# The MLP's read of tiles 4 to 15 made by GpSimd and VectorE in place of TensorE

## The reference, cut to what matters

```python
def rat_read(res, W, gamma, beta, num_outputs):      # MLP: num_outputs = 2
    x = res.reshape(b, l, H, C)                      # H = 512, C = 4
    y = jnp.einsum('blhc,hoc->bloh', x, W)           # sums of four products
    mu = y.mean(-1, keepdims=True)
    var = y.var(-1, keepdims=True)
    yn = (y - mu) * jax.lax.rsqrt(var + EPS)
    yn = yn * gamma + beta                           # per output and column
    return yn.reshape(b, l, num_outputs * H)
```

```python
delta = softplus(delta_low @ du_w.T + du_b)
A_bar = exp(delta * A_neg)                           # 1536 per token
hidden = hs * A_full + out * B_full                  # 2048 per token
```

## Time and profile before

| | us |
|---|---|
| three timed executions | 1629.28, 1638.53, 1634.19 |
| their median | 1634.19 |
| span of the profiled execution | 1627.3 |
| median less span | 6.9 |

### The profile page before, as it was taken

The page is one execution under the profiler, slowest core; times in us unless marked ns, Lnnn a source line. Parts: engine busy times, 40 slices in busy tenths (PEclk is TensorE's granted clock), DMA queues, the critical chain, the costliest instruction groups (busy, mean ns, idle before and its releaser), DMA issues.

```text
span 1627.3 us, 25328 instructions
## 1 busy us (share of the span) xinstructions
PE 1531.8 (94%) x9574; PEld 1169.6 (72%) x9574; DVE 1129.6 (69%) x1782; ACT 921.9 (57%) x1702; POOL 364.1 (22%) x346
## 2 busy tenths in 40 slices
PE   7999999999999988899999999899999999999986
PEld 6567666666666656778798778798877898875554
DVE  7777745888888878644463785974776955636777
ACT  5444345888888776455543656643657644552443
POOL 1645555555433420110002000012000011001000
PEclk8999999999999999899999999999999999999998
DMA  9667677999987945356577766667766667756542
GB/s 371 204 254 243 223 181 229 276 293 284 273 233 197 253 138 189 130 185 223 202 218 233 258 226 221 214 218 232 265 233 221 223 197 237 218 180 213 203 178 104
DMA packets 127609, 360.94 MB, mean 222 GB/s; under 512 B 15744, under 2 KB 45056, under 8 KB 111872
## 3 DMA queue, kind: packets, MB, share of 16 engines
q1 hardware_dynamic: 127200, 359.19, 68.7%
q10 hardware_dynamic: 288, 0.13, 0.0%
HBM read 273.15 MB, written 86.11 MB: 221 GB/s over the span
## 4 chain that ended last, share of the span: by engine, by line
PE 74%; DVE 12%; ACT 6%; DMA 3%; issue 3%; POOL 1%; SPq 0%; DVEq 0%; ACTq 0%; POOLq 0%
PE ps L1921 21%; PE ps L1933 9%; PE ps L693 5%; PE ps L1249 5%; PE ps L1236 4%; PE ps L1272 4%; PE ps L1946 4%; PE ps L1879 3%; PE ps L1864 3%; PE ps L1809 3%; ACT a_p L1378 3%; PE ps L1824 3%; PE ps L1891 3%; DMA p_x<-in_x 2%; PE ps L652 2%
## 5 line engine op out<-in xcount | busy, mean ns | idle before, releaser
L1921 PE MATMUL ps<-m_y_split,m_win 128*128 128x512 f32 x1536 | 372.7, 396 | 2.7 <-issue 2.7
L1921 PEld LDWEIGHTS ps<-m_y_split,m_win 128*128 128x128 f32 x1536 | 284.2, 189 | 63.9 <-issue 7.1
L1308 DVE TENSOR_REDUCE a_negmax<-ps 128x1 f32<-128x640 f32 (+7 forms) x176 | 180.7, 1027 | 61.1 <-PE ps L1239 60.3
L1378 ACT ACTIVATE a_p<-ps,a_negmax 128x128 f32<-128x128 f32 (+7 forms) x256 | 188.5, 750 | 36.0 <-DVE a_negmax L1308 33.8
L1933 PE MATMUL ps<-m_wods,m_y_split 128*128 128x316 f32 x768 | 178.7, 322 | 3.8 <-DVE m_hT L2145 3.4
L2183 ACT ACTIVATE m_turned<-ps 128x512 f32<-128x512 f32 x128 | 75.0, 596 | 160.3 <-PE ps L1809 129.1
L1249 PE MATMUL ps<-ident,a_p 128*128 128x128 f32 x1152 | 157.8, 275 | 2.9 <-DVE a_pT L1321 2.0
L1236 PE MATMUL ps<-a_k,a_q 128*128 128x512 f32 (+3 forms) x384 | 124.4, 403 | 16.7 <-ACT a_p L1378 15.0
L1933 PEld LDWEIGHTS ps<-m_wods,m_y_split 128*128 128x128 f32 x768 | 128.5, 192 | 8.0 <-DVE m_hT L2145 3.7
L1249 PEld LDWEIGHTS ps<-ident,a_p 128*128 128x128 f32 x1152 | 123.5, 141 | 5.4 <-DVE a_pT L1321 3.5
L2341 POOL TENSOR_TENSOR m_scale<-m_scale,mhalf 128x2 f32<-128x2 f32 x16 | 13.0, 813 | 493.5 <-DVE m_scale L2081 493.5
(11 more groups left out here) (250 smaller groups left out, 3095.3 us busy)
## 6 DMA issues: line engine op xcount, KB each, us to landing
m_win<-mlp_in_split SPq DMA_DIRECT2D x128, 512.0 KB, 4.4
m_wods<-mlp_out_split SPq DMA_DIRECT2D x96, 316.0 KB, 3.3
p_xT<-in_xT SPq DMA_DIRECT2D x16, 1024.0 KB, 9.9
p_x<-in_x SPq DMA_DIRECT2D x16, 1024.0 KB, 10.6
a_q<-qk_split SPq DMA_DIRECT2D x64, 256.0 KB, 7.0
a_k<-qk_split SPq DMA_DIRECT2D x128, 128.0 KB, 7.2
mlp_in_split<-a_w_two SPq DMA_DIRECT2D x32, 512.0 KB, 5.5
m_hs<-in_x SPq DMA_DIRECT2D x15, 1024.0 KB, 5.6
```

Source lines behind the costliest of these rows:

```text
L1308: V.tensor_reduce(negmax[:, n % 4, 0:len(units[n][3])], by_head(n, score_banks(n)), AX_X, ALU.max, negate=True).then_inc(max_ready, 1)
L1378: m = S.activation(dst[:, j, :], src[:, j, :], ACT.Exp, bias=negmax[:, n % 4, j:j + 1], accum_out=rsum[:, si % 2, q * 4 + hh:q * 4 + hh + 1])
L1921: m = nc.tensor.matmul(bank_of("m", blk, step), win[s][:, wl, ic, :], y[k], start=(ic == 0 and p3 == 0), stop=(ic == HCH - 1 and p3 == 2))
```

## The change

For tiles 4 to 15 the parts turn0 to turn3 and read0 to read3 go; fold0 to fold3 come in, two MLP steps apart. In fold q GpSimd multiplies quarter q of the tile (512 columns, repeated for both outputs by a zero step) with the weights `wide2[q]`, which lie in SBUF repeated over all partitions, and puts the 1024 products in `Ab[0]`; VectorE sums fours into `y2`. GpSimd's product q waits for VectorE's sum q - 1, and VectorE's sum q for GpSimd's product q. The statistics and the normalisation then work on `y2` in SBUF, in pieces of 512 columns. Tiles 0 to 3 keep the old way. The weights `wide2` are 4 KB a partition for each quarter: three loads of 512 KB in the attention stage, and one at the load of tile 4, over `read2`. To make room, the scratch that the program reserves for DMA descriptors is given as 1024.

```diff
-       'turn0': 13.72,
-       'turn1': 14.22,
-       'read0': 15.22,
-       'read1': 15.23,
-       'turn2': 15.72,
-       'turn3': 16.91,
-       'read2': 17.94,
-       'read3': 17.95,
+       'fold0': 11.2,
+       'fold1': 13.2,
+       'fold2': 15.2,
+       'fold3': 17.2,
        'stats': 17.96,
        'norm': 18.88},
...
+            for q in (1, 2, 3):
+                load_wide(q)
+
+        def load_wide(q):
+            move(wide2[q][:, :, :], read2_rows[q].unsqueeze(0).broadcast_to([P, RD2, BLK])).then_inc(wide_loaded, 16)
...
+        def folds_of(i):
+            return 4 * (i - TB + 1) if i >= TB else 0
...
             if step == "outer":
                 dve.wait_ge(dve_own.sem, own_at[what, i])
+                if lane_before[what, i] and lane_before[what, i][0] == "a":
+                    dve.wait_ge(folded, folds_of(lane_before[what, i][1]))
...
+            if part == "fold":                                  # write_dve
+                c = i % TB
+                dve.wait_ge(widened, folds_of(i) - 3 + q)
+                V.tensor_reduce(y2[c][:, :, P * q:P * q + P],
+                                Ab[0][:, 0:RD2 * BLK].rearrange("p (o h c) -> p o h c", o=RD2, c=C), AX_X,
+                                ALU.add).then_inc(folded, 1)
+            if part == "stats" and i >= TB:
+                c = i % TB
+                dve.wait_ge(folded, folds_of(i))
+                for o in range(RD2):
+                    n = dve_own.then_inc(V.bn_stats(m_st[:, c, o, 0, :], y2[c][:, o, :]))
...
             if part == "norm":                                  # write_act
                 c = i % TB
                 act.wait_ge(yscale2_ready, i + 1)
-                act.wait_ge(turn2_mm, 8 * (i // TB))
+                if i >= TB:
+                    for o in range(RD2):
+                        m = S.activation(y2[c][:, o, :], y2[c][:, o, :], ACT.Identity, bias=m_sc[:, c, 2, o:o + 1],
+                                         scale=m_sc[:, c, 1, o:o + 1])
+                    m.then_inc(y2_ready, 1)
+                    return
...
+            if part == "fold":                                  # write_pool
+                c = i % TB
+                if q == 0:
+                    pool.wait_ge(hs_ready, nth("sum", what, i))
+                    pool.wait_ge(wide_loaded, 64)
+                    pool.wait_ge(turn2_mm, 8 * (i // TB))
+                x4 = hs[hs_of[what, i]][:, BLK * q:BLK * q + BLK].unsqueeze(1).broadcast_to([P, RD2, BLK])
+                pool.wait_ge(folded, folds_of(i) - 4 + q)
+                G.tensor_tensor(Ab[0][:, 0:RD2 * BLK].rearrange("p (o f) -> p o f", o=RD2), x4, wide2[q][:, :, :],
+                                ALU.mult).then_inc(widened, 1)
...
             if part == "load":                                  # write_sp
+                if (what, i) == ("a", TB):
+                    for q2 in (2, 3):
+                        wait_for_quarter(sp, "a", TB - 1, q2)
+                    load_wide(0)
                 if hs_before[what, i]:
                     kind, j = hs_before[what, i]
                     if kind == "a":
-                        sp.wait_ge(turnq_mm, quarter["a", j, 3] + 1)
+                        if j < TB:
+                            sp.wait_ge(turnq_mm, quarter["a", j, 3] + 1)
+                        else:
+                            sp.wait_ge(folded, folds_of(j))
                         sp.wait_ge(hs_stored[h], stored["a", j])
...
-    nc = bacc.Bacc("TRN2", target_bir_lowering=False, num_devices=1)
+    nc = bacc.Bacc("TRN2", target_bir_lowering=False, num_devices=1, dynamic_dma_scratch_size=1024)
```

More of the change, by code:

```diff
@@ L262, in program @@
             read1_in, gamma1_in, beta1_in, qkvT, wod1T, wab1_b, du1_rows,
-            read2_in, gamma2_in, beta2_in, mlp_inT, wod2T, wab2_b, du2_rows,
+            read2_in, read2_rows, gamma2_in, beta2_in, mlp_inT, wod2T, wab2_b, du2_rows,
             expA, expB, br, out):
@@ L418, in program @@
         place[0] = ring_end
+        read2_place = place[0]
         read2 = sb("m_read2", [P, DCH, RD2, HPC])
+        read2_end = place[0]
         gam2 = sb("m_gamma2", [P, RD2 * HCH])
@@ L445, in program @@
         m_sc = sb("m_scale", [P, TB, 3, RD2])
+        wide2 = []
+        after, place[0] = place[0], read2_place
+        wide2.append(sb("m_read2_wide0", [P, RD2, BLK]))
+        assert place[0] == read2_end
+        place[0] = after
+        wide2 += [sb(f"m_read2_wide{q}", [P, RD2, BLK]) for q in (1, 2, 3)]
         place[0] = keep
@@ L536, in program @@
         emptied = sems("bank_emptied", 8)
-        rep1_loaded, rope_in_loaded, causal_loaded, wq_loaded, wkv_loaded = (
-            sem(n) for n in ("rep1_loaded", "rope_in_loaded", "causal_loaded", "wq_loaded",
+        rep_loaded, rope_in_loaded, causal_loaded, wq_loaded, wkv_loaded = (
+            sem(n) for n in ("rep_loaded", "rope_in_loaded", "causal_loaded", "wq_loaded",
                              "wkv_loaded"))
@@ L566, in program @@
         raw_loaded, two_stored, two_ready = sems("raw_loaded", 4), sems("two_stored", 3), sem("two_ready")
-        const2_loaded, rep2_loaded, du_loaded, du_ready = (
-            sem(n) for n in ("const2_loaded", "rep2_loaded", "du_loaded", "du_ready"))
+        const2_loaded, du_loaded, du_ready = (
+            sem(n) for n in ("const2_loaded", "du_loaded", "du_ready"))
         oT_loaded, hs_loaded, mx_loaded = sems("oT_loaded", 4), sems("hs_loaded", 6), sems("mx_loaded", 2)
@@ L585, in program @@
             sem(n) for n in ("y2_ready", "turn2_mm", "yhi_ready", "ylo_ready"))
+        wide_loaded, widened, folded = sem("wide_loaded"), sem("widened"), sem("folded")
         wt_loaded = sems("wt_loaded", NW)
@@ L729, in project_dve @@
             n48 = DCH * RD1
-            dve.wait_ge(rep1_loaded, 32)
+            dve.wait_ge(rep_loaded, 32)
             each = n48 // 3
@@ L1036, in project_sp @@
         def project_sp():
-            move(p_spread[:, :], spread_in).then_inc(rep1_loaded, 16)
-            move(wrep1[:, :], read1_in).then_inc(rep1_loaded, 16)
+            move(p_spread[:, :], spread_in).then_inc(rep_loaded, 16)
+            move(wrep1[:, :], read1_in).then_inc(rep_loaded, 16)
             def load(i):
@@ L1558, in prepare_sp @@
             move(bet2[:, :], beta2_in).then_inc(const2_loaded, 16)
-            move(m_spread[:, :], spread_in).then_inc(rep2_loaded, 16)
-            move(wrep2[:, :], read2_in).then_inc(rep2_loaded, 16)
+            move(m_spread[:, :], spread_in).then_inc(rep_loaded, 16)
+            move(wrep2[:, :], read2_in).then_inc(rep_loaded, 16)
             for k, wab in enumerate((wab1_b, wab2_b)):
@@ L1586, in prepare_dve @@
             n32 = DCH * RD2
-            dve.wait_ge(rep2_loaded, 32)
+            dve.wait_ge(rep_loaded, 64)
             V.tensor_tensor(read2[:, :, :, :].rearrange("p a b c -> p (a b) c"),
@@ L2068, in write_dve @@
                 V.tensor_tensor(hs[h][:, :], hs[h][:, :], m_x[x_at][:, :], ALU.add).then_inc(x2_ready, 1)
-            if part == "stats":
+            if part == "fold":
[9 more added lines that the diff above has]
+                    n = dve_own.then_inc(V.bn_stats(m_st[:, c, o, 0, :], y2[c][:, o, :]))
+                dve.wait_ge(dve_own.sem, n)
+                for o in range(RD2):
+                    n = dve_own.then_inc(V.bn_aggr(m_my[:, c, o, :], m_st[:, c, o, 0, :]))
+                dve.wait_ge(dve_own.sem, n)
+                V.tensor_scalar(m_sc[:, c, 0, :], m_my[:, c, :, 1], EPS, None, ALU.add).then_inc(yvar2_ready, 1)
+            if part == "stats" and i < TB:
                 c = i % TB
@@ L2411, in write_sp @@
                 move(m_x[x_at][:, :], x[i]).then_inc(mx_loaded[x_at], 16)
-            if part == "turn" and q == 0:
+            if part in ("turn", "fold") and q == 0:
                 sp.wait_ge(hs_ready, nth("sum", what, i))
@@ L2529 @@
         "read2": read_rep(L0_xattn_mlp_read_w, RD2),
+        "read2_rows": lay(np.transpose(np.reshape(L0_xattn_mlp_read_w, (4, P, RD2, C)), (0, 2, 1, 3)).reshape(4, RD2, BLK)),
         "gamma2": lay(np.reshape(L0_xattn_mlp_read_g, (RD2 * HCH, P)).T),
```

## The result

The changed kernel takes 1697.53 us (median of 4 runs, 1696.40 to 1700.18), the kernel before 1636.36 (4 runs, 1629.28 to 1638.54): 61 us slower, ratio 1.039, 95% interval 1.037 to 1.042. The profiled execution took 1697.61 with a span of 1695.5. The matmuls that the change takes away are gone, and the time went up all the same: with the 58 us of the prediction's first term, some 119 us were given back.

A forecast was written before the change was run, and what follows sets the result against it. TensorE was taken as the bound, VectorE next and on the path in dense stretches. Span 1627.3 - 19.4 + 3 - 2 - 2 = 1606.9, plus 6.9 to the runs' median: 1614 us, range 1587 to 1648.

The forecast's parts named there:

- What is removed: 58 us: First term: TensorE loses transposes and products in tiles 4 to 15, 4.8 us a tile, twelve tiles 58 us.
- GpSimd's product 2.38 us, VectorE's sum 1.2: Added per fold in tiles 4 to 15: a 1024-column product (taken 2.4 us) and a 1024-column sum (1.2 us).
- The two engines against each other: The lock: GpSimd's product holds VectorE's next operation with two SBUF inputs, up to 2.4 us a fold, 9.6 a tile.
- The sign that the prediction named for the lock: If right, VectorE's L1992 and L2021 to L2033 would show a mean above 1.76 us.
- The assumption on PSUM: VectorE operations that read PSUM keep their times while a GpSimd product runs.
- Smaller edits: SyncE at 0: SyncE's load of the next x behind fold3 costs 0, at most 4 us at tiles 10 and 14.
- The sums: 2 x 4.8 charged in dense places: VectorE's four sums, 4.8 us a tile, counted where VectorE is the path, at tiles 10 and 14.
- the waits for the product, charged only at tile 7: Tile 7's chain of folds ends late, so TensorE waits 2.4 us, taken as 3, before the first turn.
- Block 0: -16.4: Tiles 4 to 7: VectorE's free time covers the folds, -19.4 us, with 3 us of waiting after tile 7.
- Blocks 1 and 2: -2 each: Tiles 8 to 11 and 12 to 15: -19.4 + 2 + 12.8 + 2.7 = -2 us each.
- Rival 2: VectorE's in-order queue becomes the path in blocks 1 and 2; four dense tiles pay: +20, 1654 us, chance 0.25.

The follow-up runs named there:

- x12: Changed kernel with fold products and sums on a few columns, SyncE's store back at 13.72, load of the next x left at 4.08: 1589.6 us, ratio 0.973.
- x8: Changed kernel with only tiles 4 to 7 read by folds, products on VectorE, SyncE's store at 13.72 and load at 5.5, scratch 128: 1617.8 us, ratio 0.989.
- x4: Changed kernel with each GpSimd product replaced by two fills about as long that read nothing from SBUF: 1643.9 us, ratio 1.006.
- x13: Changed kernel, folds whole, with SyncE's store back at 13.72 and the load left at 4.08: 1683.9 us, ratio 1.030.
- x14: x8 with the load of the next x back at 4.08: 1617.7 us, ratio 0.990.
- x3: Changed kernel with GpSimd's products on 8 columns an output, the sums whole: 1634.4 us, ratio 1.000.
- x1: Changed kernel with products on 8 columns and 2 sums an output, same places and waits: 1618.6 us, ratio 0.991.
- x7: Changed kernel with only tiles 4 to 7 read by folds, products on GpSimd, SyncE's store at 13.72 and load at 5.5, scratch 128: 1626.5 us, ratio 0.995.
- x6: Changed kernel with VectorE making the folds' products too, SyncE's store at 13.72 and load at 5.5: 1645.4 us, ratio 1.006.
- x5: Changed kernel, folds whole, with SyncE's store at 13.72 and load of the next x at 5.5: 1687.4 us, ratio 1.032.
- x10: x8 with tiles 8 and 12 read by VectorE's folds as well: 1625.6 us, ratio 0.996.

## Why the prediction was wrong, point by point

- *What is removed: 58 us.* Right as work, and not all of it was on the path. (the earlier trace rows has sixteen products for two quarters, not eight; the 1.70 us are theirs.) x12, where the folds cost almost nothing, is 44 us below the kernel before beside it. By the starts block 0 gains 23.1 us there, more than the 19.4, and blocks 1 and 2 only 9.7 each. TensorE waits 12.3 us for "low" in x12 (4.4 in the kernel before), 7.8 for ScalarE's `m_mlp_out` (0.9) and 3.2 for weights (none); why these grow with folds of a few columns isn't shown. In block 0, x8 kept 18.1 of 19.4.
- *GpSimd's product 2.38 us, VectorE's sum 1.2.* Right (2.34 to 2.39 where undisturbed, and 1.214). The product's mean of 2.636 holds the time in which it stood behind an operation of VectorE.
- *The two engines against each other.* The mechanism was right and was read from the right rows; its size is the first step that failed. The prediction charged it only at tiles 10 and 14, 2 x 9.6 = 19 us, and took 0 elsewhere, since VectorE had free time there. Measured: 54 us (changed kernel less x4). Taking for every operation of VectorE beside a product its time above that in x4, all eight tiles from 8 to 15 pay, 4.0 to 8.3 us each, 45.6 together, and of tiles 4 to 7 only tile 6, 4.3. Free time within a stretch doesn't help there, because a product starts just as VectorE goes on to its next operations: 36 of the 48 products wait for the sum before them, and 11 for the tile's own sum (L2050). The sign that the prediction named for the lock, the operations of 1536 columns above 1.76 us, did not show: L2009, L2038, L2045 and L2050 kept their 1.76 us, and L2040 was held once (3.95 us). The held ones were others: L2028 went from 0.692 to 1.415 us in the mean, L2085 from 2.284 to 2.817. The assumption on PSUM held: all twelve operations with an operand in PSUM that lie wholly within a product (L2061, L2068, L2070, L2178) kept their times, 0.28, 0.29, 0.29 and 0.68 us.
- *Smaller edits: SyncE at 0.* The second step that failed. The prediction looked at the load behind fold3, for which SyncE waits longer (63.6 us) but which held no weights back from TensorE in x13, and whose place made no difference in x14 against x8. It never named the store, which moved from 13.72 to 11.2 with the part's name. It costs 14 us in the whole kernel, 29 with cheap folds.
- *The sums: 2 x 4.8 charged in dense places.* x3 less x1 gives 16 us; the waits for the product, charged only at tile 7, 9 more.
- *Block 0: -16.4.* Measured +0.7; the store (9, x13) and the products on GpSimd (10, x7 against x8, about half of it by the wait for tile 7's) make the difference. *Blocks 1 and 2: -2 each.* Measured +31.9 and +28.8: the lock is paid not at one dense tile in each but at all four.

The losses in one column, each the difference of two medians: lock 54 (changed - x4), waits for the product 9 (x4 - x3), sums 16 (x3 - x1), the store's early wait 29 (x1 - x12), the rest of the new order 11 (x12 less 1636.4 - 58); together the 119 to be explained. The kernel before took 1633.8 to 1636.4 beside these runs, so a term is sure to some 2 or 3 us. The split depends on the order in which the parts are taken away: the store is 29 us at the end of this column and 14 at its start.

Rival 2 named the queue that became the path and had the right side, 1654; it too priced the lock only at four tiles and knew nothing of the store. The time lies 50 us above the end of the range, 1648, and 44 above rival 2.

## What to carry to other kernels

Work moved to an idle GpSimd isn't free if both engines read SBUF: count for each product the time by which it lengthens VectorE's next two-input operation, at every tile where other work follows on VectorE and not only at the densest, and where VectorE is loose the time that it waits for the product; or let VectorE do the work itself (x6 against x5: 42 us better, x8 against x7: 9). When a part of an ordered program is renamed or moved, list everything that is issued under its name on every queue; here a store that was issued 2.5 steps earlier, and waited, held the weights behind it. Free time of an engine, averaged over a stretch, says little: a 0.3 us step that TensorE needs, behind two folds in an in-order queue, cost 8.6 us.

## What the runs showed of the hardware that was not expected

- The lock isn't one-sided: GpSimd's product stretched to 4.33 us, and its operations on one column (L2395, L2397) to 1.81 and 2.07 us, where the next pair took 0.19 and 0.55 (changed kernel, at 1087.06 and 1088.96, each beside an operation of 1536 columns on VectorE).
- GpSimd's fills are quick and hold nobody (groups of x4): 0.953 us for 1024 columns and 1.380 for 1536, and VectorE's operations kept their times: all 17 of L2028 took 0.691 to 0.694 us.

```profile
L2386 POOL MEMSET m_A<- 128x1536 f32 x48 | 66.2, 1380 | 2.8
...
L2384 POOL MEMSET m_A<- 128x1024 f32 x48 | 45.7, 953 | 285.4 <-DVE m_y L2089 150.7 <-DVE m_hs L2050 134.7
```

- VectorE's sum of fours over 1024 columns in SBUF (1.214 us) costs the same as a product of 1024 columns (1.22 us, x10).
